# Waits inside five gathered streams of a graph network kernel: the group directly in front at two columns, an older group elsewhere

## The reference

```python
edge_index = jnp.stack([src, dst])
x = x + gat(h, edge_index, ...)           # two attention convolutions, 3 heads and 1 head of 32
x = x + rgcn(h, edge_index, type_8, ...)  # two relational convolutions, 8 relations, 16->32->16
x = x + f(h) + segment_sum(w * xi * xj / (5 + 0.9 * xi + 0.1 * xj), src)
x = x + segment_sum((h[src] @ W_rel[type_90]) * e, dst)
```

## Time and profile before

| | us |
|---|---|
| median of 3 runs | 7763.85 |
| lowest, highest | 7750.85, 7764.83 |
| profiled execution: span from first to last instruction | 6645.3 |
| profiled execution's own total | not given by the page |
| POOL busy in the span | 4320.0 (65%) |
| DVE busy | 3659.5 (55%) |
| PE busy | 2965.9 (45%) |
| ACT busy | 1167.0 (18%) |

### The profile page before, as it was taken

How to read it: one execution, slowest core, us unless ns; L and a number is a source line. 1 busy time by engine, 2 the same in 40 slices (tenths; PEclk the granted TensorE clock), 3 DMA queues, 4 the chain that set the end, 5 groups by cost and what they waited for, 6 DMA issues and landing times. The chain is left out here.

```text
span 6645.3 us, 44822 instructions
## 1 busy us (share of the span) xinstructions
PE 2965.9 (45%) x13056; PEld 2260.1 (34%) x13056; DVE 3659.5 (55%) x8917; ACT 1167.0 (18%) x1912; POOL 4320.0 (65%) x3949
## 2 busy tenths in 40 slices
PE   5798699974444344447655443111111002544000
PEld 2477555543333233346644333111111001433000
DVE  8855499976555566654347667433322068876000
ACT  0265454532222233211111100000000000000000
POOL 4666555557762776376657665888888823766776
PEclk9899899985666555556667665555555555776555
DMA  2122222221110322123222212222222234211001
GB/s 41 22 62 70 56 67 67 66 66 12 20 17 14 89 60 65 47 64 100 84 87 60 64 53 72 52 36 36 44 27 27 5 96 154 57 50 37 7 7 44
DMA packets 283354, 350.11 MB, mean 53 GB/s; under 512 B 133518, under 2 KB 204432, under 8 KB 281970
## 3 DMA queue, kind: packets, MB, share of 16 engines
q1 hardware_dynamic: 112158, 295.24, 13.2%
q0 software_dynamic: 169376, 41.40, 7.8%
q10 hardware_dynamic: 1576, 10.60, 0.7%
HBM read 231.06 MB, written 122.29 MB: 53 GB/s over the span
## 5 line engine op out<-in xcount | busy, mean ns | idle before, releaser
L2352 POOL DMA_INDIRECT acc<-l_rows,l_uniq x392 | 624.1, 1592 | 121.0 <-issue 108.6
L2573 POOL DMA_INDIRECT l_ring<-t_last,idx x392 | 392.4, 1001 | 366.5 <-ACTq L2568 207.6
L521 POOL DMA_INDIRECT pay<-in_x,gidx x392 | 460.1, 1174 | 235.4 <-DMA pay<-in_x,gidx 114.3
L2393 PE MATMUL ps_l<-l_msg,l_alike 128*128 128x16 f32 x784 | 176.3, 376 | 962.4 <-DVE l_msg L2456 962.4
L1487 POOL DMA_INDIRECT g_ring<-t_gat,idx x392 | 416.1, 1062 | 278.7 <-issue 110.1
L1817 POOL DMA_INDIRECT r_ring<-t_rel,idx x392 | 414.6, 1058 | 254.6 <-issue 110.3
L809 POOL DMA_INDIRECT t_sort<-pay,c_pos x392 | 384.8, 982 | 296.3 <-DVE c_pos L875 196.3
L901 PE MATMUL ps_c<-plane,c_hit 128*128 128x400 f32 x1568 | 542.6, 499 | 1.2 <-ACT c_hit L827 1.2
L2128 POOL DMA_INDIRECT r_ring<-t_rel,idx x392 | 392.7, 1002 | 224.4 <-issue 110.4
L2338 POOL DMA_INDIRECT l_ring<-t_mix,idx x392 | 426.3, 1087 | 154.6 <-issue 119.1
L2393 PEld LDWEIGHTS ps_l<-l_msg,l_alike 128*128 128x128 f32 x784 | 171.0, 331 | 967.7 <-DVE l_msg L2456 967.7
(11 more groups left out here) (529 smaller groups left out, 8145.0 us busy)
## 6 DMA issues: line engine op xcount, KB each, us to landing
c_rows_d<-row_dst SPq DMA_DIRECT2D x98, 256.0 KB, 3.3
l_keys<-row_at SPq DMA_DIRECT2D x49, 512.0 KB, 4.2
l_typs<-row_typ SPq DMA_DIRECT2D x49, 512.0 KB, 3.7
g_hs<-t_gat SPq DMA_DIRECT2D x30, 660.0 KB, 4.7
acc<-r_zero SPq DMA_DIRECT2D x60, 320.0 KB
t_rel<-r_row SPq DMA_DIRECT2D x30, 640.0 KB, 3.5
r_hs<-t_rel SPq DMA_DIRECT2D x30, 640.0 KB, 4.7
d_gain<-acc SPq DMA_DIRECT2D x30, 640.0 KB, 6.0
```

The source lines that it names most:

```text
L521: pool.indirect_dma_start(pay[:, s, 8:PAY], None, x, bass.IndirectOffsetOnAxis(gidx[:, s:s + 1], 0)).then_inc(gat_in[s // BATCH], 16)
L2352: pool.indirect_dma_start(acc[r], bass.IndirectOffsetOnAxis(uniq[:, s:s + 1], 0), rows[:, (s // ES) % RR, s % ES, :], None, compute_op=ALU.add
L2573: pool.indirect_dma_start(ring[:, s, :], None, t_last, bass.IndirectOffsetOnAxis(idx2[:, s:s + 1], 0)).then_inc(gat_in[s // BATCH], 16)
```

## The change

For s = 0, 160 and 320 POOL waits for the group directly in front (none exists at 0); at every other eighth column for the group two back. BATCH, RUN, the gathers, the consumers and their waits stay.

```diff
-    n = s // BATCH - (1 if s >= RUN else 2)
+    n = s // BATCH - (1 if s % RUN == 0 else 2)
     if s % BATCH == 0 and n >= first // BATCH:
         engine.wait_ge(landing[n], 16 * BATCH)
```

## The result

The changed kernel takes 7967.98 us (median of 4; 7963.88 to 7985.15), the kernel before 7764.34 us in the same comparison (7750.85 to 7792.03). The ratio is 1.0262, 95% interval 1.023 to 1.0294. I had forecast 7568, with a range of 7538 to 7612.

The account below looks back on a forecast made before the run. POOL's gather stream, with its waits, was taken to bound G1, G2, R2 and L3, and R1's late part until PE's products do. Savings 28.7 + 31.9 + 30.2 + 64.6 + 40.0 = 195.4 us gave 7568 us, range 7538 to 7612.

Parts of the forecast that it names:

- I take the other 1118.55 us of the 7763.85 median as unchanged: Whole kernel: the sum was made against the 6645.3 us span, the rest of the measured time assumed untouched.
- columns 72 to 151 of each stream already run in this form, and their rate has such accidents in it: Five gather streams: these loosely paced columns' rates were taken to include occasional costly waits, some 3 us for a few.
- R1: Stage where PE's products become the bound: 18 late steps drop to 10.65 us each, saving 30.2 us.
- G1: Stage paced by POOL's gathers: 26 removed waits at 1.10 us each save 28.7 us.
- G2: Stage paced by POOL's gathers: 23 removed waits at 1.39 us each save 31.9 us.
- R2: Stage where PE waits for gathers: 27 removed waits at 2.39 us each save 64.6 us, all on the path.
- L3: Stage that ends when POOL's scatters end: 27 removed waits at 1.48 us each save 40.0 us.
- C: G2, R1, R2: denser gathers delay 90 chunk loads; at 5 us each, 8018 us; chance with any other loss 0.04.
- D: Streams: nothing moves, 7764 us, as long loose runs stall by themselves, or 7629 with three stalls a stream; chance 0.07.
- A: R1: POOL sets its pace to the end, the rest by wait lengths; 233 us saved, 7531; chance 0.12.
- B: G1 and G2: DVE becomes the bound and each gives half, 30 us less gain in all, 7599; chance 0.14.
- The lock of the shared port: POOL's streams: VectorE holding the port blocks GpSimd's descriptor writes; terms 195 us with it, 208 by wait lengths alone.

Follow-up runs that it names:

- e9: The kernel before, unchanged, run again for a profile in a job where it is slow: 7836.10 us, ratio 1.0038.
- kind B: The one job, on its own chip, in which the kernel before, unchanged, took 6633 us.
- kind A: The four jobs, each on another chip, in which the kernel before, unchanged, took 7753 to 7824 us, as in the first comparison.
- e3: Against the kernel before, POOL waits for the group two back at every eighth column, never the one in front: 6438.60 us, ratio 0.9705 (kind B).
- e1: The kernel before, unchanged, run again for a profile of a timed run: 6639.03 us, ratio 1.0004 (kind B).
- e4: Against the kernel before, only R1's stream paced in the new form, the other four as before: 6613.91 us, ratio 0.9967 (kind B).
- e5: The changed kernel, unaltered, run again: 7976.91 us, ratio 1.0176 to the kernel before (kind A).
- e7: Against the kernel before, waits two back everywhere, with three linked POOL memsets behind each: 6875.60 us, ratio on record 0.8759 (kind A).
- e11: Against the kernel before, POOL waits for the group in front at the second column of each eight: 7974.24 us, ratio 1.0214 (kind A).
- e10: Against the kernel before, waits for the group in front at every sixteenth column, two back at other eighths: 7706.58 us, ratio 0.9864 (kind A).

## Why the prediction was wrong

- **The step that failed is the first one: "I take the other 1118.55 us of the 7763.85 median as unchanged".** Nothing lay outside the span. The trace was of a chip where the kernel takes 6633 us, the times of chips where it takes 7764, and the 1118 us stood inside the five stages (e9: 1114 us more in them than in the trace, of the 1160 us by which its span is longer). That every later span lies within 2 us of its own time shows the first; that the trace was of such a chip follows from its length, which only kind B has.
- **With it fell "columns 72 to 151 of each stream already run in this form, and their rate has such accidents in it".** They do run in this form, and on kind A they are where the execution starves. POOL's own rate does not show it: POOL is faster there (99.86 us for R1's 80 columns, against 107.02). Who pays are the others, and on kind B they don't.
- **What the change costs on kind A.** The waits of the kernel before at columns 160 to 384 brought G1 back to pace before its stream ended, and in G2 and R2 they kept the others at pace behind the stop at column 280; the change took them away. I had priced them by what they cost POOL alone. Changed against e9: G1 +79, G2 +41, R1 0, R2 +76, L3 and scatters -8 us, together 188; with -15 us ahead of G1 and +4 in the third layer they make the 178 us by which the two spans differ. R1 lost nothing because there the waits of before had never freed anyone.
- **The working itself holds on kind B, in the main.** Loose against the trace, with my terms in brackets: G1 -34.9 (-28.7), G2 -33.0 (-31.9), R1 -29.1 (-30.2), R2 -63.6 (-64.6), L3 with the scatters -45.4 (-40.0); 195 us by medians (195.4). e3 is not quite the changed kernel: that has two blocking waits more a stream, an estimated 5 x 2 x 1.4 = 14 us, so the gain there would be some 181 us and not 195, and my terms are a little high. The changed kernel itself did not run on kind B, so 6450 us there is an estimate. R1 did turn to PE as its bound, with no wait of DVE for a gather, but that its term fits to 1 us is luck: it stands on the one trace whose R1 took 627.3 us. Against e1's 619.7, e3 gives 21.5, and run alone (e4) the change gave 19. (R2's busy 1.002 us a column is over 160 columns, L3's 1.007 over 161; over 161 it is 0.996, and nothing hangs on it.)
- **Rivals.** C had the right sign, the wrong mechanism: it priced late loads, and its point of decision (2.2 us a load) was never tested by anything. ACT and DVE wait for PE, and PE waits for a loaded chunk (`r_hs`) 1.6 and 15.8 us in all in R1 and R2, as before (1.7 and 15.8). D named the unpaced scatter's stalls; no stream of the changed kernel shows an "issue" stall above 0.9 us. A and B moved the gain by 38 and 30 us, and kind B speaks against both: R1 gave 19 to 29 us and not 55, G1 and G2 their full terms. The 9.9 and 14.0 us by which I argued for A are the longest of 7 and of 10 waits; the means, 9.7 and 13.7, say the same. I gave everything slower 0.03: I searched for a mechanism in a trace in which it does not happen.
- **The lock of the shared port** from the Trainium skill, "SBUF — State Buffer", section "SBUF: two separate sides", was a matter of 13 us (rates against wait lengths). e3's 195 us, and more so the 181 estimated for the changed kernel, is nearer to the rates' 195 than to 208, but no run separates the lock from other causes. It is not what the 204 us went to: in R1's window DVE, which would hold the lock, ran nothing at all (0.00 us in 99.86).

**What stays open.** Why jobs differ in this, and whether it is the chip. What in POOL's stream holds PE's signals back. Whether a result is there before its signal: the ends of matmuls in the profile are modelled, and the trace shows only that PE has begun other matmuls by then. That it is PE's signal is read from the traces of R1 and from no experiment. What 1.7 us of standing still at every eighth column has that 0.8 us, or 1.7 us at every sixteenth, has not. Why G1 recovered under the waits in e9 and R1 did not.

## What to carry to other kernels

Compare the span with the measured time before pricing anything: here they differed by 1118 us in the one case and by under 2 us in all others, and the rates of that trace did not hold for the timed executions. A wait that costs its own engine time may be what lets the others run, so price a removed wait on all engines, and in a trace that belongs to the timed executions. Of the forms that ran, waiting for the group in front at every eighth column is the safe one: 6801 and 6813 us on either kind, 13% faster than before where before starves, 2.5% slower where it doesn't; the fully loose form is the fastest on kind B (6439) and among the slowest on kind A (7978).

## What the runs showed of the hardware that I had not expected

- In four of the five jobs, each on another chip, and in the first comparison, a stream of indirect DMAs that POOL issues every 1.25 us without pause holds back the engines that wait for PE: 32 PE matmuls in 99.9 us of R1, where the same program makes 338 in 107.0 on another chip. Behind the stream they run at once (228 in 100 us).
- In that state PE's semaphore is raised 19 to 63 us behind the matmuls, against 0.02 us outside it, and ACT follows it by 0.02 us. ACT's copies at 3550.18 and 3561.38 start 42 and 52 us after the matmuls that they wait for, and its starts lie on a beat: these two are 11.20 us apart, and in the same stage of e5 one finds 3525.49, 3536.69 and 3547.89.
- A pause of 1.3 us (memsets) or 1.7 us (a landing) at every eighth column keeps the others going, the first not always (R2 in e7); 0.4 to 0.8 us at every eighth (e11) does not, nor does 1.7 us at every sixteenth, apart from G2 (e10).
- Once starved, a stage can stay so through 29 such pauses (R1 of e9), or recover after some 230 us of them (G1 of e9). A stop of POOL for 32 to 50 us at column 280 freed G2 and R2 in both kernels; it lasted to the end of the stream with the waits, without them to about column 362 in G2 and for fewer than 40 columns in R2.
- The stream of indirect DMAs with no wait for landings at all (line 809) stops at its 114th column, in the changed kernel for 4.1 us again; in those of the changed kernel that wait no "issue" stop is above 0.9 us.
